# Cross attention and a mixture of experts on one core: unrolled expert loops, another order of value tile and key sum, prefix sums by two products

## What is computed

```python
# attention: 32 heads of 16, q and k normalised per head, no softmax maximum needed
x = x + xattn(layernorm(x), ctx, Wq, Wk, Wv)
# experts
xt = layernorm(x).reshape(2048, 512)
gate = xt @ Wr + br                        # 7 routed experts
ids = top_2(gate + gate_bias)
probs = softmax over the two chosen gates  # zero elsewhere
for each routed expert e and a shared one:
    u = xt @ Wup[e] + bup[e]
    g = silu(u @ Wgate[e] + bgate[e]) * u
    eo[e] = g @ Wdown[e] + bdown[e]
x = x + sum_e probs[:, e] * eo[e] + eo[shared]
```

## Time and profile before

| | us |
|---|---|
| median of 3 runs | 982.45 (982.33 to 983.61) |
| the profiled execution | 984.33 |
| its span | 982.6 |
| attention and its start | 0 to about 467 |
| shared expert, tiles 0 to 7 | about 467 to 610 |
| routed tiles, 20 | about 610 to 971 |
| last reading of y, scatter, end | 971.15 to 982.6 |

### The profile page before, as it was taken

How to read it: one execution, slowest core, us unless ns; L and a number is a source line. 1 busy time by engine, 2 the same in 40 slices (tenths; PEclk the granted TensorE clock), 3 DMA queues, 4 the chain that set the end, 5 groups by cost and what they waited for, 6 DMA issues and landing times.

```text
span 982.6 us, 18038 instructions
## 1 busy us (share of the span) xinstructions
PE 952.8 (97%) x6720; PEld 685.5 (70%) x6721; DVE 707.1 (72%) x1460; ACT 497.6 (51%) x619; POOL 203.3 (21%) x209
## 2 busy tenths in 40 slices
PE   7999999999999999999999999999999999999995
PEld 6633443454443553345989998999989999999995
DVE  6798667876778757885968985855857576858653
ACT  4588568866787568887333222422424243424221
POOL 1011000311012200321100000333233333233331
PEclk9999999999999999999999999999999999999998
DMA  9400100100201020223411242543644536635523
GB/s 331 163 1 22 65 1 1 44 33 12 86 2 43 38 71 1 83 79 102 189 66 44 75 156 97 159 109 53 177 83 103 143 76 190 183 66 152 120 52 41
DMA packets 32217, 86.28 MB, mean 88 GB/s; under 512 B 7712, under 2 KB 7712, under 8 KB 28064
## 3 DMA queue, kind: packets, MB, share of 16 engines
q1 hardware_dynamic: 21632, 59.65, 16.9%
q0 software_dynamic: 10528, 25.87, 13.1%
HBM read 61.83 MB, written 23.67 MB: 87 GB/s over the span
## 4 chain that ended last, share of the span: by engine, by line
PE 85%; DVE 10%; issue 2%; DMA 1%; ACT 1%; DVEq 0%; POOLq 0%; SPq 0%; POOL 0%; ACTq 0%
PE z_ps L875 16%; PE y_ps L875 15%; PE u_ps L875 15%; PE o_ps L611 10%; PE scores L595 7%; PE bank_b L632 5%; PE bank_a L648 4%; PE bank_b L618 2%; PE xt_ps L887 2%; PE bank_a L618 2%; PE tr L671 2%; PE tr L666 1%; PE tr L677 1%; DMA ctx_raw<-ctx_t 1%; DVE k_lo L1390 1%
## 5 line engine op out<-in xcount | busy, mean ns | idle before, releaser
L1144 ACT ACTIVATE probs<-scores 128x2048 f32<-128x2048 f32 x128 | 240.7, 1880 | 77.6 <-PE scores L595 74.6
L875 PE MATMUL z_ps<-u_hi,w_sb 128*128 128x256 f32 x896 | 167.9, 285 | 1.4 <-DVE u_lo L1819 1.4
L875 PE MATMUL u_ps<-x_hi,w_sb 128*128 128x256 f32 x864 | 159.4, 283 | 3.0 <-issue 3.0
L1174 ACT ACTIVATE u_hi<-u_ps,b_ug 128x256 fp32r<-128x256 f32 x108 | 45.4, 471 | 199.9 <-PE u_ps L875 199.9
L875 PEld LDWEIGHTS z_ps<-u_hi,w_sb 128*128 128x128 f32 x896 | 140.6, 190 | 2.7 <-DVE u_lo L1819 1.8
L875 PE MATMUL y_ps<-w_sb,g_hi 128*128 128x512 f32 x448 | 139.5, 392 | 0.0
L875 PEld LDWEIGHTS u_ps<-x_hi,w_sb 128*128 128x128 f32 x864 | 135.5, 190 | 5.5 <-issue 4.5
L611 PE MATMUL o_ps<-probs,v_sb 128*17 128x512 f32 x1024 | 136.4, 605 | 0.0
L875 PE MATMUL z_ps<-u_lo,w_sb 128*128 128x256 f32 x448 | 126.3, 282 | 0.0
L875 PE MATMUL u_ps<-x_lo,w_sb 128*128 128x256 f32 x432 | 121.9, 282 | 0.0
L1186 ACT ACTIVATE s_sb<-z_ps,b_ug 128x256 f32<-128x256 f32 x112 | 47.1, 472 | 105.7 <-PE z_ps L875 105.7
(11 more groups left out here) (246 smaller groups left out, 1579.6 us busy)
## 6 DMA issues: line engine op xcount, KB each, us to landing
w_raw<-w_all SPq DMA_DIRECT2D x27, 1024.0 KB, 6.9
ctx_raw<-ctx_t SPq DMA_DIRECT2D x4, 1024.0 KB, 7.3
out<-x_sb SPq DMA_DIRECT2D x16, 256.0 KB, 2.0
x_sb<-x SPq DMA_DIRECT2D x1, 3072.0 KB, 16.2
xn<-x_t SPq DMA_DIRECT2D x12, 256.0 KB, 4.4
xn_dram<-xn SPq DMA_DIRECT2D x12, 256.0 KB, 2.1
xt_dram<-xt SPq DMA_DIRECT2D x6, 512.0 KB, 3.0
xg<-xt_dram POOLq DMA_DIRECT2D x10, 256.0 KB, 3.2
```

Source lines behind the costliest of these rows:

```text
L875: ins = nc.tensor.matmul(out_ps, stat[a], mov[b], start=(first and a + b == 0), stop=(last and a == 1), skip_group_check=True)
L1144: nc.scalar.activation(probs[:, t % 2], scores[:], ACT.Exp).then_inc(p_ready, 1)
L1174: last = nc.scalar.activation(u_hi[:, c, :], u_ps[:, b, a, :], ACT.Identity, bias=b_ug[:, par, 0, c:c + 1])
```

## The change

1. In attention, in units with g = 2 that have a next batch, the value tile now comes ahead of `sum_k` on PE, both behind `weighed`, and DVE reads the value tile ahead of the sum.
2. The splits of three quarters of the shared expert's down weights move: quarter 1 from unit 12 step 7 to unit 13 step 6, quarter 2 from unit 13 step 6 to unit 14 step 2, and of quarter 3 (unit 13 step 7) the high part goes to ACT, the low part to unit 14 step 3.
3. The prefix sums are made otherwise: `tile_totals` makes the total of each tile and expert as one column, DVE copies it (`totals_out`), and one product of that column, broadcast, with a 0-1 matrix adds the totals to all tiles behind. POOL makes the matrix (`tile_order`) with 16 `affine_select`.
4. The routing's DVE work is spread anew over tiles 2 to 7, with the splits of expert 1's weights.
5. SP stores the transposed tokens of the last batch to `xt_dram` from `place`; tiles 6 and 7 are loaded from there (`NT` = 8), without PE's transposes. ACT's last split of expert 1 waits for the stores, since it writes over `place`. Expert 2's weights are loaded one matrix at a time.
6. PE, ACT and DVE run the experts unrolled, with all seven bounds loaded into registers ahead: on PE behind the quarters of y in tiles 5 and 6, on ACT and DVE in tile 7's `during_y`. POOL and SP keep the loop of pairs.
7. In a routed tile DVE writes bias times share into `y_sb` ahead of y's arrival, and reads y with one instruction for each half.

```diff
-        NT = (TILES - BT) // 2
+        NT = NA
...
+        def experts(engine, start_at, head, tile, first_tile=None):
+            for j in range(1, ER + 1):
+                head(j, j % 2, j // 2)
+                first = start_at[j - 1]
+                if first_tile is not None:
+                    first_tile(j, first + NA, j % 2)
+                    first = first + 1
+                with engine.Fori(first, start_at[j]) as i:
+                    tile(i + NA, j % 2, j)
+
+        def bound(engine, e):
+            return engine.value_load(start_i[0:1, e:e + 1], min_val=0, max_val=MOST)
...
+            nc.gpsimd.memset(tile_order, 0.0).then_inc(order_set, 1)
+            for t in range(1, TILES + 1):
+                pool.wait_ge(order_set, t)
+                nc.gpsimd.affine_select(out=tile_order, in_=tile_order, compare_op=ALU.not_equal, fill=1.0,
+                                        base=-ER * t, pattern=[[1, (TILES + 1) * ER]], channel_multiplier=-1)\
+                  .then_inc(order_set, 1)
...
+            for t in range(0, BT, 2):
+                sp.wait_ge(t2_done, t + 2)
+                sp.dma_start(xt_dram[(TILES - BT + t) // 2], place[:, t:t + 2]).then_inc(xt_stored, 16)
...
-                elif t == 11:
-                    sp.wait_ge(lo_done, 6)
-                    load_weights(2)
+                elif t in (5, 13, 15):
+                    load_weight(2, (5, 13, 15).index(t))
...
-                    if u + 1 < UNITS:
+                    if u + 1 < UNITS and not (more and g == 2):
                         sum_k(u + 1)
...
                 if s == 2 and more and g == 2:
                     v_even(u)
+                    sum_k(u + 1)
...
-                for t in range(TILES):
-                    behind = [P, TILES - t, ER]
-                    last = nc.tensor.matmul(at[:, t + 1:, :], ones[:], picked[:, t:t + 1, :].to_broadcast(behind),
-                                            start=False, stop=(t == TILES - 1), skip_group_check=True)
-                last.then_inc(window_ready, 1)
+                nc.tensor.matmul(xt_ps[0:TILES * ER, 1, 0, 0:1], picked[:, 0:TILES, :].rearrange("p t e -> p (t e)"),
+                                 ones[:, 0:1], start=True, stop=True, skip_group_check=True).then_inc(totals_ready, 1)
...
+                nc.tensor.matmul(at, totals[0:TILES * ER, 0:1].to_broadcast([TILES * ER, P]), tile_order[0:TILES * ER],
+                                 start=False, stop=True, skip_group_check=True).then_inc(window_ready, 1)
...
-            tile(3, 0, behind_up=lambda: prefixes(3), windows=1)
+            tile(3, 0, behind_up=tile_totals, behind_z=prefixes)
...
+            tile(5, 0, behind_up=lambda: table_part(5, 0), windows=2, bounds=range(1, DC + 1))
+            tile(6, 0, behind_up=lambda: table_part(6, 1), windows=3, bounds=range(DC + 1, ER + 1))
...
+            experts(pe, start_at, lambda j, par, nth: pe.wait_ge(lo_done, j * 6), tile)
...
-                elif at == (-4, 7):
+                elif at == (-3, 6):
                     first_weight(2, 1)
-                elif at == (-3, 6):
+                elif at == (-2, 2):
                     first_weight(2, 2)
-                elif at == (-3, 7):
-                    first_weight(2, 3)
+                elif at == (-2, 3):
+                    first_weight_low(2, 3)
...
+                    for h in range(2):
+                        nc.vector.tensor_scalar(y_sb[:, h, :], bd[:, par, :], row_now[:, h, j - 1:j], None, ALU.mult)\
+                          .then_inc(y_biased, 1)
...
+                        nc.vector.scalar_tensor_tensor(at, y_v[:, h, :], row_now[:, h, j - 1:j], at, ALU.mult,
+                                                       ALU.add).then_inc(y_done, 1)
...
-            tile(3, 0, x_tile=6, during_u=splits(1, 1, [0]), before_x=prefixes_out, during_z=probabilities,
-                 during_y=steps_of(starts, positions))
-            tile(4, 0, x_tile=8, during_u=lambda: hot_rows(0),
-                 during_y=steps_of(lambda: hot_cols(0), lambda: hot_rows(1)))
-            tile(5, 0, x_tile=10, during_u=splits(1, 1, [1]), before_x=lambda: table_out(0), during_y=lambda: hot_cols(1))
+            tile(3, 0, x_tile=6, before_x=totals_out, during_z=probabilities, during_y=steps_of(prefixes_out, starts))
+            tile(4, 0, x_tile=8, during_u=positions, during_y=lambda: hot_rows(0))
+            tile(5, 0, x_tile=10, during_u=lambda: hot_cols(0), before_x=lambda: table_out(0),
+                 during_y=lambda: hot_rows(1))
...
+            tile(6, 0, x_tile=12, during_u=lambda: hot_cols(1), before_x=lambda: table_out(1),
+                 during_y=splits(1, 1, [1]))
...
+            tile(7, 0, x_tile=14, during_u=last_split, during_y=bounds)
```

More of the change, by code:

```diff
@@ L967, in tile @@
                             last.then_inc(y_ready, 1)
+                    if c < len(bounds):
+                        start_at.append(bound(pe, bounds[c]))
             tile(0, 0, amid_z=lambda: out_transposes(UNITS - 1, 1))
@@ L1200, in _, with bounds, head @@
             tile(2, 0, during_y=splits(1, 1, [1]))
-            tile(3, 0, during_z=choice_exp, during_y=splits(1, 1, [2]))
-            for n in range(4, NA):
+            tile(3, 0, during_z=choice_exp, during_y=last_high)
+            for n in range(4, NA - 1):
                 tile(n, 0)
-            def head(j, par, nth, first):
+            start_at = [0]
+            def bounds():
+                act.wait_ge(start_ready, 1)
+                for e in range(1, ER + 1):
+                    start_at.append(bound(act, e))
+            tile(NA - 1, 0, during_y=bounds)
+            def head(j, par, nth):
                 act.wait_ge(b_loaded[par], nth * 32 + 32)
@@ L1220, in first_tile @@
                     tile(n, par, before_u=one, during_z=lambda: split(j + 1, 1 - par, 1, [0]), during_y=rest)
-            routed(act, head, tile, first_tile)
+            experts(act, start_at, head, tile, first_tile)
         @block.vector
@@ L1515, in step @@
                         v_out(0, 2)
-                    if more and g == 3:
+                    if more and g >= 2:
                         v_out(b + 1, 2 * g - 4)
@@ L1906, in first_tile @@
                          during_z=lambda: split(j + 1, 1 - par, 1, [0]), during_y=rest)
-            routed(dve, head, tile, first_tile)
+            experts(dve, start_at, head, tile, first_tile)
 def kernel(**inputs):
```

99 lines of the change are left out of this document (55 added, 44 removed).

## The result

The changed kernel took 973.0 us (median of 4 runs, 972.38 to 973.43), the kernel before 982.9 beside it; the ratio is 0.9899, 95% interval 0.9881 to 0.9916. The prediction said 967.5, with a range of 963.5 to 972: the sign was right, and a third of the gain was missing, 9.9 us in place of 15.0. The profiled execution took 973.43, its span is 971.7 against 982.6, 10.9 us less.

The account below looks back on a forecast made before the run. TensorE (PE), busy 97% of the span, was taken to bound the kernel. The terms -8.2, -0.35, -3.1, -0.6, +1.8, -1.8, -2.2, 0 and -0.5 sum to -15.0 us: 982.45 to 967.5 us, range 963.5 to 972.

Parts of the forecast that it names:

- Value tile ahead of key's sum: Attention units 2, 6, 10: PE's idle time before `sum_k` and the clock loss behind it go; -8.2 us, bounds -4.7 and -8.6.
- First weights: Units 13 and 14: moved splits close two PE holes, -1.15, but PE waits 0.8 later; -0.35 us, bounds -1.15 and +0.65.
- The wait of 0.8 at the output's transposes: Unit 14: three more DVE instructions ahead of `norm2_out` make PE wait about 0.8 us at the output's transposes.
- Prefix sums: Tile 3: three short products replace one of 0.21 and 16 of together 3.48 us; -3.1 us, bounds -3.3 and -2.0.
- routing's spread: Tile 4: with `positions` moved there, DVE reads tile 3's y earlier and PE's hole at `u_lo` shrinks; -0.6 us.
- hot_cols: Tiles 5 and 6: moved into the u phase, it makes PE's `table_part` wait 0.9 us each; +1.8 us, bounds 0 and +2.4.
- x^T: Tiles 6 and 7: loading through DRAM saves PE's eight transposes, 0.91 us on the chain for each tile; -1.8 us.
- Unrolled: Starts of the second and third expert pairs: PE's "issue" waits of about 1.1 us go; -2.2 us, bounds 0 and -2.6.
- rival of jumps: Unrolled experts: jumps or first visits cost PE; unrolling brings nothing, 977 us (chance 0.06), or slower, 991.7 us (0.04).
- Into expert 1: Entry to expert 1: DVE's seven bounds loads leave `u_lo` starting as late as before; 0 us, bounds -0.8 and +0.8.
- PE waits for `u_lo` over 1 us: Sign expected in the trace at the entry to expert 1: PE waits over 1 us for `u_lo`.
- Bias times share: Routed tiles: bias scaled while PE is in y; on the chain one scale before the last scatter goes, -0.5 us.

Follow-up runs that it names:

- sixteen sums: The changed kernel with the prefix sums' second product made as before by 16 products, one per tile of tokens: 976.1 us, ratio 0.9923.
- late bounds: The changed kernel with DVE loading only experts 1 and 2's bounds ahead of reading tile 7's y, later ones at each expert's head: 968.4 us, ratio 0.9854.
- loads added: The kernel before with seven unused loads of bounds added on DVE ahead of the reading of tile 7's y: 984.9 us, ratio 1.0020.
- weights wait: The changed kernel with one wait added on SyncE, so expert 3's weight loads are asked for only once tile 10's gathered tokens have come: 967.4 us, ratio 0.9849.

## Why the prediction was right or wrong, point by point

- **Value tile ahead of key's sum, -8.2: right in these two traces** (units 2, 6, 10: -3.06, -1.87, -3.47 = -8.4). The wait of 0.4 behind the logarithm came (0.55). The clock's share in it is the less certain part: unit 10's 1.6 was lost in both traces of the old attention code, but not when the old order was put back into the changed kernel.
- **First weights, -0.35: a little better.** Units 13 and 14 are 0.6 and 0.3 shorter. The wait of 0.8 at the output's transposes was 0.17; DVE's row of before has 2.0 us of gaps between the sum and that copy, where I had counted 1.
- **Prefix sums -3.1 and routing's spread -0.6: -3.3 together in the trace, -3.0 for the products** by the run with sixteen sums. The spread gave 0.3 in place of 0.6.
- **hot_cols +1.8, x^T -1.8: right in sign and place** (two waits of 0.89, and none of the 0.91 for transposes); the two tiles came out 0.4 longer, not equal.
- **Unrolled, -2.2: right** (-2.2 from tile 10 to the last, +2.15 there when undone). No rival of jumps came.
- **Into expert 1, 0: the step that failed.** It read: "3.0 push the reading of y, and 2.7 to 3 go behind it. `u_lo` starts as late as before. **0**". For `u_lo` that was a little too cautious: the seven loads took 4.2 us and not 4.9, and pushed the reading of y by 2.4 and not 3.0; `u_lo` started 1.1 us earlier, tiles 7 and 8 gained that, and the sign "PE waits for `u_lo` over 1 us" did not come (0.54). That is a matter of size. The zero failed because I followed the reading of y only along DVE's own row. The sum that this step makes has another reader, SP, which stores the sum, and behind SP stand POOL's scatter and gather. I checked expert 2's weights against their reader and never asked what expert 3's, which I had not touched, would meet when the gather slid toward them. The runs showed in its place a wait of 3.99 us for tile 10's tokens and 1.5 us of lower clock behind it, 5.5 in tile 9, all of it gone when the loads wait for the gather. The trace of before had the leads: gather issued at 625.76, weights at 630.78, use at 635.14. A push of 2.4 and the 1.1 that the tiles gain leave 1.5 us over the weights and about 6 to the use. With the 7.67 us that the gather took in the run with late bounds at a lead of 1.2, I estimate a wait of some 1.6 us from these two alone. The other 2.5, between the reading of y and the gather's issue, I could not have read there.
- **Bias times share -0.5**: -0.8.

The forecast's mechanisms outside that step sum to what was measured with the collision removed: 967.4, against 967.5. That near-equality is partly luck, since attention gave 1.1 more, 0.5 of it ahead of the first exponential, and the tiles up to 6 gave less.

Open: why the way from reading y to the gather's issue was 2.5 us longer. It is 16.64 and 16.96 us in the two traces with the kernel before's code and 17.3 to 18.4 in the eleven runs on the changed code, so most of it comes with that code; POOL's index copy, 1.28 us in the changed kernel and 0.19 to 0.96 in the others, is the part that varies. Open too: why the clock fell behind a wait of 1.81 us in tile 9 of one run and not behind 1.94 in that of another.

## What to carry to other kernels

When a step is moved on one engine, follow every reader of its result to the end, across the engines that only move data: here DVE, SP, POOL, the DMA engines, then PE, 20 us later. A transfer's slack is the smaller of two distances, to its use and to the next large transfer on the same DMA engines; here the second was spent first, the gather's duration doubled (3.9 us to 7.6), and the wait came at once. Here the cure was to hold the prefetch with time to spare behind the small transfer that had none.

## What the runs showed of the hardware

- The same idle time of 1.58 us ahead of `sum_k` was followed by a granted clock of 0.50 (1.2 GHz) in unit 2 of all three traces with the old order, in unit 10 of two of them (the kernel before, and that kernel with loads added), and in unit 6 of none. In tile 9 a wait of 1.81 us was followed by 0.50, one of 1.94 by 1.00 throughout. PE's idle time alone doesn't tell whether the clock falls.
- The second half of a gather, 128 rows, was in 3.9 us after its issue with the three 1 MB loads held back (weights wait). In all seven traces in which the loads were issued between 1.0 us before it and 1.2 us behind it, it took 7.4 to 8.2 us.
- An indirect scatter with no other transfer beside it (tile 10's in the changed kernel, 660 to 665 us) keeps the 16 DMA engines at a mean share of 0.84 with only 105 GB/s; with weight loads in flight they moved 425 GB/s at 1.02.
- Seven loads of bounds on DVE cost 4.2 us of its row, each about 0.3 for the load (298 to 551 ns) and 0.18 for the register operation behind it.
